# Layer norms of a fused transformer kernel's second cross attention, moved between engines

## What is computed

```python
x = x + tanh(g_xattn[0]) * L0_xattn(layernorm(x), ctx, Wq, Wkv)
x = x + tanh(g_ffn[0])   * L0_ffn(layernorm(x), Wr, Wqkv, Wo)        # tokens chosen per expert, attention among them
x = x + tanh(g_xattn[1]) * L1_xattn(layernorm(x), ctx, ctx, mask, Wq, Wk, Wv, Wo)   # 16 heads, 32 keys
x = x + tanh(g_ffn[1])   * L1_ffn(layernorm(x), ln_gamma, ln_beta, router_w, ...)   # top 2 of 8 experts + a shared one

# inside L1_ffn
mu = mean(xt); var = mean((xt - mu)**2)
normed = (xt - mu) * rsqrt(var + LN_EPS) * ln_gamma + ln_beta
probs = softmax(normed @ router_w.T); top_v, top_i = top_k(probs, 2)
```

## Time and profile before

| | us |
|---|---|
| median of 3 runs (331.44 to 333.52) | 331.97 |
| the profiled execution, its own time | 333.4 |
| its span, first to last instruction | 331.6 |
| busy in the span: PE / DVE / ACT / POOL | 246.3 / 221.9 / 195.1 / 168.4 |
| mean granted TensorE clock | 0.892 of full |
| stage of the second cross attention and routing, to the last send | about 118 to 221 |

### The profile page before, as it was taken

The page is one execution under the profiler, slowest core; times in us unless marked ns, Lnnn a source line. Parts: engine busy times, 40 slices in busy tenths (PEclk is TensorE's granted clock), DMA queues, the critical chain, the costliest instruction groups (busy, mean ns, idle before and its releaser), DMA issues.

```text
span 331.6 us, 6994 instructions
## 1 busy us (share of the span) xinstructions
PE 246.3 (74%) x2113; PEld 188.1 (57%) x2113; DVE 221.9 (67%) x687; ACT 195.1 (59%) x454; POOL 168.4 (51%) x208
## 2 busy tenths in 40 slices
PE   2887770797999788998987925414999999998600
PEld 2773240355777465677756712212799999997400
DVE  2487078995677666688899766700577767676555
ACT  2753599687677688976864444200676666764220
POOL 2513199931222564741106777750068888787521
PEclk9999996799999999999999555755999999999965
DMA  7880003420000000000000111433123222211093
GB/s 202 239 354 6 1 1 123 141 102 0 3 1 2 0 3 1 2 0 2 1 2 33 42 41 54 124 100 81 35 74 91 76 61 82 78 37 32 1 285 95
DMA packets 21458, 21.64 MB, mean 65 GB/s; under 512 B 3360, under 2 KB 19106, under 8 KB 20784
## 3 DMA queue, kind: packets, MB, share of 16 engines
q1 hardware_dynamic: 18784, 16.79, 16.8%
q0 software_dynamic: 2496, 4.26, 4.0%
q10 hardware_dynamic: 144, 0.15, 0.2%
HBM read 14.68 MB, written 7.42 MB: 67 GB/s over the span
## 4 chain that ended last, share of the span: by engine, by line
PE 31%; POOL 19%; DVE 19%; issue 15%; ACT 7%; DMA 5%; SPq 0%; POOLq 0%; DVEq 0%; ACTq 0%
PE bank L1148 25%; POOL expert_rows L818 12%; POOL dispatched_rows L794 6%; DVE region_p L897 2%; DVE x L1139 2%; DVE region_k L884 2%; DMA region_q<-expert_rows 2%; DVE top L883 2%; DVE nm L970 1%; DVE region_k L972 1%; DMA dispatched_rows<-region_t,slot 1%; PE bank L1355 1%; POOL rstd L736 1%; DVE bn_raw L843 1%; DMA x<-in 1%
## 5 line engine op out<-in xcount | busy, mean ns | idle before, releaser
L1148 PE MATMUL bank<-w_scaled,w_high 128*128 128x256 f16 x276 | 48.2, 279 | 1.0 <-ACT w_scaled L689 1.0
L818 POOL DMA_INDIRECT expert_rows<-region_k,slot_dest x24 | 29.5, 1229 | 28.1 <-DVE region_k L1121 21.1
L794 POOL DMA_INDIRECT dispatched_rows<-region_t,slot x32 | 32.6, 1019 | 16.6 <-issue 9.2
L1148 PE MATMUL bank<-w_high,region_k 128*128 (+1 forms) x308 | 32.3, 224 | 8.5 <-DVE region_k L1088 7.0
L1148 PE MATMUL bank<-w_scaled,w_low 128*128 128x256 f16 x138 | 38.4, 278 | 0.0
L689 ACT ACTIVATE w_scaled<-bank 128x512 f16<-128x512 f16 x23 | 13.7, 597 | 38.0 <-PE bank L1450 37.9
L1124 DVE TENSOR_TENSOR region_k<-region_x,region_k 128x768 f16<-128x768 f32 x23 | 22.0, 958 | 19.0 <-ACT region_k L694 19.0
L1148 PEld LDWEIGHTS bank<-w_high,region_k 128*128 128x128 f16 x308 | 25.7, 100 | 10.9 <-DVE region_k L1088 8.4
L818 POOL DMA_INDIRECT expert_rows<-region_x,slot_dest x22 | 27.3, 1241 | 6.7 <-issue 6.7
L745 POOL TENSOR_TENSOR w_low<-w_scaled,w_high 128x512 f16<-128x512 f32 (+1 forms) x23 | 27.8, 1236 | 5.5 <-ACT w_high L523 5.3
L1148 PEld LDWEIGHTS bank<-w_scaled,w_high 128*128 x276 | 26.5, 100 | 4.5 <-issue 1.3
(11 more groups left out here) (236 smaller groups left out, 708.5 us busy)
## 6 DMA issues: line engine op xcount, KB each, us to landing
w_scaled<-in SPq DMA_DIRECT2D x5, 1024.0 KB, 8.2
w_scaled<-dispatched_rows SPq DMA_DIRECT2D x23, 131.0 KB, 2.3
region_q<-expert_rows SPq DMA_DIRECT2D x4, 512.0 KB, 5.6
dispatched_rows<-pad_rows SPq DMA_DIRECT2D x18, 65.5 KB, 2.7
x<-in SPq DMA_DIRECT2D x4, 256.0 KB, 4.5
region_w<-in SPq DMA_DIRECT2D x2, 512.0 KB, 7.3
out<-x SPq DMA_DIRECT2D x4, 256.0 KB, 2.5
w_scaled<-in SPq DMA_DIRECT2D x1, 704.0 KB, 4.1
```

The costliest lines, as they stand in the source:

```text
L794: pool.indirect_dma_start(disp, bass.IndirectOffsetOnAxis(slot[:, b * T + t, c:c + 1].bitcast(U32), 0), pay[:, b * T + t, :], None).then_i ...
L818: pool.indirect_dma_start(ytok, bass.IndirectOffsetOnAxis(dst[:, n, h:h + 1].bitcast(U32), 0), yv[n % 4][:, h * D:(h + 1) * D], None, boun ...
L1148: return pe.matmul(o, l, r, start=start, stop=stop)
```

## The change

The first norm of all four batches leaves ACT. POOL makes it right behind `rstd`, one `tensor_scalar` per tile (times rstd, plus the negative mean times rstd), with a signal for each. The second norm of batches 0 and 1 (`POOLED = 2`) leaves ACT, and its gamma and beta leave DVE: POOL makes all of it behind `rstd2`, four `tensor_scalar` and two `tensor_tensor` of 128x512. Batches 2 and 3 keep the second norm on ACT and DVE. All waits for the results stay where they are: PE's `xt` waits for each tile, ACT's `high` waits for `ffn_affine`.

```diff
+POOLED = 2
@@ ACT
-                elif stage == "first_norm" and t == 0 or stage == "norm" and t % T == 0 and t > 0:
-                    act.wait_ge(pre1_rstd, b + 1)
-                    for u in range(t, t + T):
-                        act.activation(xh[:, u, :], x[:, u, :], ACT.Identity, bias=nmr[:, u:u + 1],
-                                       scale=rstd[:, u:u + 1]).then_inc(pre1_normed, 1)
-                elif stage == "norm2" and t % T == T - 1:
+                elif stage == "norm2" and t % T == T - 1 and b >= POOLED:
                     normalise(b, ffn_rstd, ffn_normed)
@@ POOL
                 if stage == "rstd" and t % T == 0:
                     rstd_of(b, pre1_stats, pre1_rstd)
+                    pool.wait_ge(pre1_rstd, b + 1)
+                    pool.wait_ge(slot_mixed, NX)
+                    for u in range(t, t + T):
+                        pool.tensor_scalar(xh[:, u, :], x[:, u, :], rstd[:, u:u + 1], nmr[:, u:u + 1], ALU.mult,
+                                           ALU.add).then_inc(pre1_normed, 1)
...
                 elif stage == "rstd2" and t % T == T - 1:
                     rstd_of(b, ffn_stats, ffn_rstd)
+                    if b < POOLED:
+                        n = slice(b * T, (b + 1) * T)
+                        pool.wait_ge(ffn_rstd, b + 1)
+                        pool.wait_ge(pre1_turned, (b + 1) * T)
+                        for u in range(b * T, (b + 1) * T):
+                            last = pool.tensor_scalar(xh[:, u, :], x[:, u, :], rstd[:, u:u + 1], nmr[:, u:u + 1], ALU.mult, ALU.add)
+                        link(last)
+                        link(pool.tensor_tensor(xh[:, n, :], xh[:, n, :],
+                                                gamma[:, :].rearrange("p (a d) -> p a d", a=1).to_broadcast((P, T, D)), ALU.mult))
+                        pool.tensor_tensor(xh[:, n, :], xh[:, n, :],
+                                           beta[:, :].rearrange("p (a d) -> p a d", a=1).to_broadcast((P, T, D)),
+                                           ALU.add).then_inc(ffn_affine, 1)
@@ DVE
-                elif stage == "affine" and t % T == T - 1:
-                    dve.wait_ge(ffn_normed, b + 1)
+                elif stage == "affine" and t % T == T - 1 and b >= POOLED:
+                    dve.wait_ge(ffn_normed, b + 1 - POOLED)
```

## The result

| | before | changed |
|---|---|---|
| median of 20 executions each, us | 332.50 | 335.65 |
| lowest to highest | 330.29 to 334.67 | 332.16 to 338.66 |
| the profiled execution's span | 331.6 | 333.5 |

The ratio is 1.0069, with a 95% interval of 1.0041 to 1.0097: slower by 2.3 us by the ratio, 3.15 by the medians, where 1.4 us less were forecast. The time lies above the range of 329.0 to 333.6. The ratios of this text leave out executions over 1.5% above their kernel's fastest and the medians don't, so where a kernel spreads, as this one does, the ratio's difference is the smaller; I give both where it matters. The kernel before ran again beside each series of experiments, with medians of 331.97, 332.00 and 331.43; a difference "by the medians" is taken from before's median of the same series.

A forecast was written before the change was run, and what follows sets the result against it. POOL's queue up to the last send was taken as the bound, paced before 174 by ACT and DVE. 0.95 + 0.97 - 0.5 = 1.4 us earlier gave a median of 330.5, range 329.0 to 333.6.

The forecast's parts named there:

- step 1: First norm of batch 0: with ACT freed, tile 0's transpose is copied earlier for PE; gain 0.63 us.
- step 2: First norm of batch 1: tile 2's exponential no longer waits for ACT; 0.45 us earlier, PE using about 0.4.
- The price of POOL's chain: Second norm of a batch on POOL: 1.85, 4 x 0.30, 2 x 1.04 and three semaphore turns, 5.4 us.
- Step 3: Second norm of batch 0: ACT's `high` waits for POOL, PE idles about 1 us anew, gain stays at 0.95.
- Step 4: Second norm of batch 1: DVE's next shift starts 0.97 us earlier; up to 0.9 more on POOL is free.
- Step 5: POOL's norms of batch 1 against DVE's `route` of batch 0: mutual waits of 0 to 1.5 us, taken as 0.5.
- the clock rival: New idle near 155 halves PE's clock for two tiles: some 5 us more, about 336; chance 0.07.
- The slower-POOL rival: At ACT's `high` of batches 0 and 1, POOL's norm becomes the hold: +3.4 us, 335.3; chance 0.10.

The follow-up runs named there:

- the fill: Changed kernel plus ten unread 128x512 fp16 matmuls in PE's queue ahead of the transpose of tile 11: 331.05 us, ratio 0.9986.
- batch 1's norm alone: Changed kernel with batch 0's second norm back on ACT and DVE; first norms and batch 1's second norm on POOL: 329.44 us, ratio 0.9955, the lowest median.
- the hold: Kernel before plus five unread 128x512 fp16 copies on ACT ahead of batch 0's `high`, no norm on POOL: 336.22 us, ratio 1.0139.
- both kernels with the ten products: Ten unread matmuls ahead of tile 11's transpose, in the changed kernel (331.05 us) and in the kernel before with five copies on ACT (332.45 us).
- the first norms alone: Changed kernel with both second norms back on ACT and DVE, only the first norms on POOL: 330.91 us, ratio 0.9986.
- `high` behind the copy: Changed kernel with two slots moved, `high` 8.6 to 9.0 and `low` 8.9 to 9.1, so ACT copies tile 10's transpose first: 332.84 us, ratio 1.002.
- the fills with a late wait: Unread matmuls ahead of `w` and scores of tile 13: batch 1's-norm-only version 338.71 us, kernel before 342.58, reordered changed kernel 336.82.

## Why the prediction was wrong, by its steps

**Steps 1 and 2 were right.** PE's second transpose of the stage:

```profile
121.40 0.30 PE L1380 MATMUL bank<-c,x_hat 128*128 128x128 f32 x1 [0.46 <-ACT region_x L648]
```

Its idle is 0.46 instead of 1.07, so 0.61 for the 0.63 of step 1; up to batch 0's statistics it is 0.80 where 0.95 was forecast, so step 2 was worth 0.2 rather than 0.4.

**The price of POOL's chain was 1.0 short**: 6.38 for 5.4. The four tiles took 1.75 where 1.20 was put (0.55 more), the two passes 2.53 where 2.08 was put (0.45 more); the small instructions ahead took 0.09 more and the turns 0.08 less. The trace of before had closer rows than the one I took, and they stood on its page and in its groups by line:

```profile
L745 POOL TENSOR_TENSOR w_low<-w_scaled,w_high 128x512 f16<-128x512 f32 x22 | 26.9, 1251 | 5.5 <-ACT w_high L523 5.3
...
L828 POOL TENSOR_TENSOR x<-x,region_q 128x512 f32<-128x512 f32 x2 | 2.6, 1324 | 8.5 <-ACT region_q L708 8.4
```

Both have two different tiles as inputs and neither is a broadcast of a few columns, and they say 1.25 and 1.32 (L745's mean takes in eight that ran beside DVE's passes; those from 116 us on take 1.16 in the median). The row I took, L785, has two broadcast operands and said 1.04. The Trainium skill's "GPSIMD Engine Reference" (section Engine selection), which I weighed and passed over, puts two-input operations at about twice DVE's time; by that factor my estimate was 1.36 for a pass and 6.0 for the chain. Measured, 1.27 on POOL against 0.68 on DVE is a factor of 1.9, so the trace now agrees with it.

**Step 3**: the kind was right, the size wrong. Expected was an idle of 1 us before tile 11's transpose and a gain kept; with 1.0 us more on POOL it became 2.35. Where the clock doesn't fall (the fill), batch 1's statistics come 0.28 late instead of 0.80 early: 1.08 lost, which is about the 1.0 of the chain.

**Step 4 was right**: from batch 1's statistics to the first send the fill kernel gains 0.88 of the 0.97, and `high` of batch 1, in the changed kernel's ACT row below, waits 0.88 for POOL. It waits as long in the kernel with batch 1's norm alone, whose first send comes 0.91 earlier than before.

```profile
172.69 0.63 ACT L651 ACTIVATE region_t<-x_hat 128x512 f16<-128x512 f32 x1 [0.88 <-POOL x_hat L815]
```

**Step 5 was wrong, on the safe side.** It took 0.5 for POOL and DVE being in each other's way during `route`. POOL's four tiles of batch 1 and two of DVE's operations in that time, in the changed kernel:

```profile
168.14 1.82 POOL L811 TENSOR_SCALAR x_hat<-x,rstd,minus_mean_rstd 128x128 f32<-128x128 f32 x4
```

```profile
168.00 0.17 DVE L1033 CAST expert_of<-r_idx 128x8 f32<-128x8 uint32 x1
...
168.28 0.22 DVE L1035 TENSOR_TENSOR one_hot<-c,expert_of 128x64 f32<-128x64 f32 x1
```

POOL's take 1.82 against 1.75 alone, DVE's keep their 0.17 to 0.22, and from the cast to the next shift DVE takes 1.09 here (168.00 to 169.09) and took 1.09 before (166.50 to 167.59). That is 0.07 on POOL and nothing on DVE. The doubling in the earlier trace rows is that of passes of 512 columns. By the Trainium skill's "SBUF — State Buffer" (section Who interferes with whom) the one-hot operation, with two inputs in SBUF, would be locked against POOL's reads; no delay of it can be seen here.

So the sum without the clock is -0.80 + 1.08 - 0.88 = -0.60 at the first send, and the fill kernel, in which all the rest of the change is there, shows 53.10 against 53.70 and a median 0.9 under that of before, 0.5 by the ratio, which its interval doesn't tell from none. My -1.4 was 0.8 too good (0.15 by step 2, 1.08 by the chain's price, 0.09 by step 4, less the 0.5 of step 5), and that alone would have left the time in the range.

**The step that failed is step 3's "The gain stays at 0.95": the new idle was priced at its own length, and the clock behind it at nothing.** What decided was the rival I gave 0.07. Its price was near: "some 5, about 336", and 335.65 was measured; in the profile 3.27 us of it stand at batch 1's statistics (3.55 less the 0.28 that the stall makes alone) and another 1 at the first send, from the second spell, 4.3 together. That the median came so near 336 is in part luck: the 5 was added to a base that was itself 0.8 too good. The first piece is shown to come from the idle and the slow clock behind it, by the fill (same stall, no idle, no spell) and by the hold; for the second piece the clock is read from the windows, and what started that spell isn't shown, though it is gone in both kernels with the ten products. Its chance was wrong, for two reasons that could have been seen. The evidence against it was that idles of 0.83 and 1.07 had left the clock at 1.00; but they are at most as long as the one that I was forecasting in the same text, and say nothing of a longer one; and behind the 1.25 before 181.33, which I named, the clock did go to 0.50. And I tied the idle to the term least known. The stall was the difference of two near numbers (155.7 from POOL against 155.7 from PE, plus the copies), so each 0.1 us on POOL is 0.1 us of idle; with the upper half of my own bounds for POOL it is over 2. The slower-POOL rival did reckon with such a stall, but priced it one for one; the clock rival did not ask what POOL's price does to it. Taken together they are one case: "POOL's chain over 6", worth about 4 to 5 us by the clock and not 1. It needed a chance of its own, and not a small one.

What stays open: why one execution with an idle of 2.33 kept its clock; and what starts the spells at 166 to 178, which came in both profiles of the changed kernel, in those of the first norms alone (0.85 and 0.72), of batch 1's norm (0.64, 0.51), of `high` behind the copy (0.57) and of the hold (0.85, 0.72), and not in that of before. Of these kernels the first norms alone and batch 1's norm have no long idle ahead of it and are no slower than before in the median, so this spell by itself doesn't explain the changed kernel's loss. The fill in the fastest kernel, placed in an idle without a wait of its own, wasn't tried.

## What to carry to other kernels

Before work goes to a slower engine, follow what stands in the queue behind the wait for it: if TensorE's next operand is there, the stall can be paid a second time in clock, here 1 us of stall and some 3 to 4 us lost at half speed behind it. Move the piece whose consumer has slack (batch 1's norm, ahead of the send) and leave the one whose consumer is in front of TensorE's next tile (batch 0's). And a rival's chance is to be read at the sizes that the forecast itself allows, not at those of the trace before.

## What the runs showed of the hardware

- TensorE at half clock behind an idle of 2.1 to 3.0 us, in five of six profiled executions, with full clock behind the idles of 0.83 to 1.54 at the same place; ten products nobody reads, in the idle, kept it at 1.00 and gave back 3.5 to 3.8 us in one pair of kernels and 2.8 to 4.1 in the other. Further on, three idles of 1.85 and 1.86 (the fills with a late wait) had slow spells beside them too, in a stretch where such spells also came beside an idle of 0.63 or 0.64, in six of ten profiles; and behind idles of 1.25 to 1.29 near the stage's end in all.
- POOL: 128x512 f32 `tensor_tensor` 1.04 us with one tile on both inputs or with two small broadcast operands, 1.26 to 1.29 with a full tile and gamma; `tensor_scalar` of 128x128 0.30 (constants, bf16 out), 0.38 (f32 out), 0.45 (two pointer scalars), and 0.69 with one pointer scalar and no second operation, more than with two.
